# Attention head groups closed by VectorE straight out of PSUM, with the reciprocals and the last pass's preparing steps moved

## What is computed

```python
# layer 1, on x (8, 512, 512); 16 heads of 32
q, k, v = split(layernorm(x) @ w_qkv);  q, k = rotary(q), rotary(k)
attn = softmax(where(causal, q @ k.T / sqrt(32), -inf))
x = x + layernorm((attn @ v) @ w_o)
# layer 2, on z = layernorm(x)
h = z + attention(rmsnorm(z))        # latent keys and queries, again 16 heads of 32
out = h + moe(rmsnorm(h))            # 1 shared and 7 routed experts, top 2
x = x + layernorm(out)
```

## Time and profile before

| | |
|---|---|
| runs of the kernel before | 2252.98, 2257.77, 2262.41 us; median 2257.77 |
| the profiled execution | 2260.6 us, of which the span from first to last instruction is 2258.9 |
| PE busy | 2058.7 us (91%) |
| DVE, ACT, POOL busy | 1527.8 (68%), 1047.8 (46%), 1066.4 (47%) |
| attention stage | to about 1656 us of the span |
| mean granted clock of PE | 0.963 of full speed |

### The profile page before, as it was taken

How to read it: one execution, slowest core, us unless ns; L and a number is a source line. 1 busy time by engine, 2 the same in 40 slices (tenths; PEclk the granted TensorE clock), 3 DMA queues, 4 the chain that set the end, 5 groups by cost and what they waited for, 6 DMA issues and landing times. The chain is left out here.

```text
span 2258.9 us, 38261 instructions
## 1 busy us (share of the span) xinstructions
PE 2058.7 (91%) x12760; PEld 1471.1 (65%) x12760; DVE 1527.8 (68%) x4267; ACT 1047.8 (46%) x2154; POOL 1066.4 (47%) x1103
## 2 busy tenths in 40 slices
PE   5899989999998999999899999989689999999994
PEld 5676555767655576765557676555356778888883
DVE  5676777776666777666677776667646656565657
ACT  2345454443445444344543434454424355656554
POOL 1455654645555463555546455554525522323237
PEclk9999999999998999999899999989799999999997
DMA  5555556655545665555566555544446889999887
GB/s 174 172 138 150 151 150 178 188 135 139 160 140 150 177 189 133 140 158 143 150 168 197 149 143 153 147 113 117 136 164 243 282 233 241 214 225 234 218 238 258
DMA packets 227632, 394.74 MB, mean 175 GB/s; under 512 B 24942, under 2 KB 96238, under 8 KB 226158
## 3 DMA queue, kind: packets, MB, share of 16 engines
q1 hardware_dynamic: 164638, 294.69, 45.0%
q0 software_dynamic: 16064, 36.84, 8.8%
q10 hardware_dynamic: 46736, 60.77, 8.0%
HBM read 144.68 MB, written 146.35 MB: 129 GB/s over the span
## 5 line engine op out<-in xcount | busy, mean ns | idle before, releaser
L1044 DVE CUSTOM_DVE_ANT_0 unused<-score,mask 128x128 bf16<-128x128 f32 (+3 forms) x1024 | 468.3, 487 | 263.3 <-PE score L1280 245.6
L792 ACT ACTIVATE probs<-scoresT 128x512 f32<-128x512 f32 (+3 forms) x1024 | 426.5, 437 | 468.5 <-PE scoresT L1303 453.5
L1303 PE MATMUL scoresT<-stacks 97*128 97x256 f32 (+2 forms) x1024 | 399.0, 404 | 37.4 <-ACT probs L792 26.2
L697 POOL TENSOR_TENSOR probs<-probs 128x1536 f32<-128x1536 f32 (+1 forms) x128 | 375.1, 2931 | 34.1 <-PE out_ps L1317 24.8
L1280 PE MATMUL score<-stacks 96*128 96x256 f32 (+2 forms) x1024 | 347.9, 385 | 20.8 <-DVE rowmax L1044 17.8
L1162 PE MATMUL middle<-weights_by_part,xh 128*128 128x256 f32 x1792 | 343.9, 287 | 6.4 <-DVE weights_by_part L1013 4.6
L686 POOL TENSOR_SCALAR_AFFINE_SELECT probs<-probs 128x512 f32<-128x512 f32 x256 | 164.8, 644 | 345.1 <-ACT probs L792 345.1
L2510 PE MATMUL into<-xh,weights_by_part 128*128 128x512 f32 (+1 forms) x960 | 301.6, 382 | 4.5 <-PEq L468 2.4
L1162 PEld LDWEIGHTS middle<-weights_by_part,xh 128*128 128x128 f32 x1792 | 291.1, 192 | 17.6 <-DVE weights_by_part L1013 5.3
L1303 PEld LDWEIGHTS scoresT<-stacks 97*128 97x128 f32 x1024 | 195.5, 194 | 161.7 <-ACT probs L792 92.7
L1280 PEld LDWEIGHTS score<-stacks 96*128 96x128 f32 x1024 | 183.7, 195 | 152.8 <-issue 116.6
(11 more groups left out here) (233 smaller groups left out, 3242.5 us busy)
## 6 DMA issues: line engine op xcount, KB each, us to landing
stacks<-rows SPq DMA_DIRECT2D x768, 128.0 KB, 2.4
x_slots<-mask ACTq DMA_DIRECT2D x57, 1032.0 KB, 5.3
rows<-in_L_attn_x SPq DMA_DIRECT2D x16, 1024.0 KB, 5.8
weights_by_part<-parts_kept SPq DMA_DIRECT2D x7, 2048.0 KB, 8.8
raw<-in_gates SPq DMA_DIRECT2D x24, 512.0 KB, 6.7
raw<-in_ups SPq DMA_DIRECT2D x24, 512.0 KB, 5.9
raw<-in_downs SPq DMA_DIRECT2D x24, 512.0 KB, 6.8
rows<-x_slots SPq DMA_DIRECT2D x11, 1032.0 KB, 7.1
```

The costliest lines, as they stand in the source:

```text
L697: pool.tensor_tensor(probs[0][:, :, P * j:T], probs[0][:, :, P * j:T], probs[j][:, :, :], ALU.add)\
L792: act.activation(probs[j][:, h, 0:width], scoresT[:, u % ST_BANKS, first:first + width], ACT.Exp, scale=SCALE).then_inc(exp_done, 1)
L1044: ins = dve.tensor_tensor_reduce(unused[t][:, :], score.bank(name)[:, first:first + width], mask[:, T - width:T], 1.0, MASKED, ALU.add, AL ...
L1303: pe.matmul(scoresT[:, u % ST_BANKS, 0:T - first], heads[0:ROWMAX + 1, 1, h, j * P:(j + 1) * P], heads[0:ROWMAX + 1, 0, h, first:T], start ...
```

## The change

It does this:

- `O` and `CL` are gone, and with them `taken`, `whole`, `take_output` on ACT and `close` on POOL. `close` is now on DVE: one product of 128x512, `out_ps` by `total` into `outT`, right behind reciprocal 3. `close_last` takes `out_ps` for its four products too.
- The reciprocals are due at shares 0, 0.05, 0.10, 0.15 in every group. `PV` 0, 1, 2 move forward by 0.02.
- The next group's `PV` 0 and reciprocal 0 wait for DVE's product (`multiplied`) in place of `taken` and the old `out_done`.
- In pass 15: loading the first rows of h (`EF`) moves to the start of group 61; `EQ` 0 to the start of group 62, `EN` 0 after eight rooms, `EL` behind it; `EQ` 1 and `EN` 1 behind all of group 63's steps, ahead of its reciprocals.
- Just ahead of `PV` 2 of group 63, PE does the first three of four quarters of `Y` for row tiles 0 and 1.

```diff
@@ projections_between
+            if not starts:
+                steps = [("EF",)] + steps
@@
-            return [("EL",)] + [room] * AHEAD_AT[0] + [("EQ", 0)] + [room] * AHEAD_AT[1] + [("EN", 0)] + [room] * AHEAD_AT[2]
+            return [("EQ", 0)] + [room] * AHEAD_AT[0] + [("EN", 0), ("EL",)] + [room] * AHEAD_AT[1]
@@
-        steps += [room] * AHEAD_AT[3] + [*(("XT", p, k) for k in range(CT)), ("EQ", 1)] + [room] * AHEAD_AT[4]
+        steps += [room] * AHEAD_AT[3] + [("XT", p, k) for k in range(CT)] + [room] * AHEAD_AT[4]
         for k in range(CHUNKS):
             steps += [("EW", k), room]
-        steps += [("EN", 1)]
@@ head_group
-        steps += [(0.0, ("O", n - 1)), *((0.05 + (0.08 if n % NG else 0.04) * t, ("I", n - 1, t)) for t in range(TT))]
-    if n % NG > 0:
-        steps += [(0.45, ("CL", n - 1))]
+        steps += [(0.05 * t, ("I", n - 1, t)) for t in range(TT)]
@@
-    steps += [(share, ("PV", n, j)) for j, share in enumerate((0.37, 0.55, 0.74))]
+    steps += [(share, ("PV", n, j)) for j, share in enumerate((0.35, 0.53, 0.72))]
@@ attention_order
+            if step == ("PV", last, 2):
+                yield from quarters("Y", f, 0)[:3] + quarters("Y", f, 1)[:3]
+            yield step
+    yield from [("EQ", 1), ("EN", 1)]
     for t in range(TT):
-        yield "I", n, t
+        yield "I", last, t
     for t in range(TT):
-        yield from quarters("Y", f, t)
+        yield from quarters("Y", f, t)[3 if t < 2 else 0:]
@@ semaphores
+        def multiplied(n):
+            if n % NG == NG - 1:
+                return last_done, TT * (n // NG + 1)
+            return out_done, (NG - 1) * (n // NG) + n % NG + 1
@@ sync
+                def load_first():
+                    sp.wait_ge(h_stored, stores_of_h(max(opened(blocks)[:Ahead.OPENINGS]) + 1))
+                    sp.wait_ge(*middle.full(("XT", cores - 1, CT - 1)))
+                    sp.dma_start(normed[:, :, :], h_out[opened(blocks)[0]:opened(blocks)[0] + 1, :, :].rearrange(in_rows, p=P)).then_inc(qkv_in, 16)
@@ gpsimd: close and its call removed;  scalar: take_output and its call removed
@@ vector
-                        if n % NG > 0:
-                            dve.wait_ge(out_done, closed_by_pool(n))
-                        elif n > 0:
-                            dve.wait_ge(last_done, TT * (n // NG))
+                        if n > 0:
+                            dve.wait_ge(*multiplied(n - 1))
@@
+                def close(n):
+                    out_free(n)
+                    dve.wait_ge(inverted, TT * (n + 1))
+                    dve.tensor_tensor(outT[:, n % OUTS, :], out_ps[:, :], total[:, :], ALU.mult).then_inc(out_done, 1)
@@ close_last
-                    dve.tensor_tensor(outT[:, n % OUTS, mine], whole[:, mine], total[:, mine], ALU.mult)\
+                    dve.tensor_tensor(outT[:, n % OUTS, mine], out_ps[:, mine], total[:, mine], ALU.mult)\
@@
+                    if step == "I" and which[0] % NG < NG - 1 and which[1] == TT - 1:
+                        close(which[0])
@@ tensor, times_v
-                        pe.wait_ge(taken, n)
+                        pe.wait_ge(*multiplied(n - 1))
```

More of the change, by code:

```diff
@@ L271, in attention_order @@
     groups = NG * cores
+    f, last = cores - 1, groups - 1
     for n in range(groups):
-        yield from merged(head_group(n, groups), projections_between(n // NG, n % NG, cores))
-    f, n = cores - 1, groups - 1
-    yield "O", n
+        for step in merged(head_group(n, groups), projections_between(n // NG, n % NG, cores)):
+            if step == ("PV", last, 2):
+                yield from quarters("Y", f, 0)[:3] + quarters("Y", f, 1)[:3]
+            yield step
+    yield from [("EQ", 1), ("EN", 1)]
     for t in range(TT):
-        yield "I", n, t
+        yield "I", last, t
     for t in range(TT):
-        yield from quarters("Y", f, t)
+        yield from quarters("Y", f, t)[3 if t < 2 else 0:]
     yield "HS", f
@@ L374, in attention_layers @@
         total = sb("total", [P, T])
-        whole = sb("whole", [P, T])
         unused = [sb(f"unused{t}", [P, P * (t + 1)], BF16) for t in range(TT)]
@@ L443, in attention_layers @@
         sum_done = semaphore("sum_done")
-        taken = semaphore("taken")
         inverted = semaphore("inverted")
@@ L447, in attention_layers @@
         last_done = semaphore("last_done")
-        def closed_by_pool(n):
-            return (NG - 1) * (n // NG) + n % NG
+        def multiplied(n):
+            if n % NG == NG - 1:
+                return last_done, TT * (n // NG + 1)
+            return out_done, (NG - 1) * (n // NG) + n % NG + 1
         def half_turned(n, which):
@@ L588, in _ @@
                 for step, *which in order:
+                    if step == "EF":
+                        load_first()
                     if step == "EL":
@@ L698, in add @@
                         .then_inc(added, 1)
[L700 to L707, removed]
                 def scale_ahead(o):
@@ L735, in _ @@
                         x1_roots(*which)
-                    if step == "CL":
-                        close(*which)
             @block.scalar
@@ L793, in exps @@
                                    ACT.Exp, scale=SCALE).then_inc(exp_done, 1)
-                def take_output(n):
-                    if n % NG > 0:
-                        act.wait_ge(out_done, closed_by_pool(n))
-                    elif n > 0:
-                        act.wait_ge(last_done, TT * (n // NG))
-                    act.wait_ge(pv_done, TT * (n + 1))
-                    act.activation(whole[:, :], out_ps[:, :], ACT.Copy).then_inc(taken, 1)
                 def plain_keys(n):
@@ L862, in _ @@
                         take_high(*which)
-                    if step == "O":
-                        take_output(*which)
                     if step == "PV" and which[1] == 1 and which[0] <= NR * blocks:
@@ L1056, in invert, with out_free @@
                         dve.wait_ge(sum_done, n + 1)
-                        if n % NG > 0:
-                            dve.wait_ge(out_done, closed_by_pool(n))
-                        elif n > 0:
-                            dve.wait_ge(last_done, TT * (n // NG))
+                        if n > 0:
+                            dve.wait_ge(*multiplied(n - 1))
                     dve.reciprocal(total[:, mine], sum_ps[:, mine]).then_inc(inverted, 1)
+                def out_free(n):
+                    if n == 1:
+                        dve.wait_ge(parts_stored, 48)
+                    if n >= OUTS:
+                        dve.wait_ge(*middle.full(("Y", (n - OUTS) // NG, TT - 1)))
+                def close(n):
+                    out_free(n)
+                    dve.wait_ge(inverted, TT * (n + 1))
+                    dve.tensor_tensor(outT[:, n % OUTS, :], out_ps[:, :], total[:, :], ALU.mult).then_inc(out_done, 1)
                 def close_last(n, t):
                     mine = slice(t * P, (t + 1) * P)
[L1066 to L1069, removed]
                     if t == 0:
-                        dve.wait_ge(taken, n + 1)
+                        out_free(n)
                     dve.wait_ge(inverted, TT * n + t + 1)
-                    dve.tensor_tensor(outT[:, n % OUTS, mine], whole[:, mine], total[:, mine], ALU.mult)\
+                    dve.tensor_tensor(outT[:, n % OUTS, mine], out_ps[:, mine], total[:, mine], ALU.mult)\
                        .then_inc(last_done, 1)
```

2 lines of the change are left out of this document (removed).

## The result

The changed kernel took 2225.39 us (median of four runs, 2221.03 to 2232.09) against 2257.43 us for the kernel before in the same series (four runs, 2252.98 to 2262.41). The ratio is 0.9856, with a 95% interval of 0.9837 to 0.9875: 32 us faster, where 11 were forecast and 2229 us was the low end of the range. The profiled execution took 2225.16 us, 1.8 more than its span of 2223.4, against 2260.6 before. The expert stage is the same block as before (602.4 us against 602.3, from its first instruction on POOL to the end of the span), so the question is the attention stage alone. It ended 35.7 us earlier, at 1620.95 instead of 1656.61.

A forecast was written before the change was run, and what follows sets the result against it. The body was taken as bound by PE with small gaps, the stage's end by chains between engines. Body -3.1 and end -8.0 made -11.1 us, 2246.7 on the median, rounded to 2246; forecast 2238 to 2252, range 2229 to 2262.

The forecast's parts named there:

- ACT's copy: Body: removing 64 copies of 598 ns on ACT gains 1 us (bounds 0 and 5).
- POOL's product: Body: without 48 products on POOL the cut ends earlier and PV 2 waits less, 6.5 us gained (bounds 4 and 8).
- The clock behind it: Body: half clock behind three late PV 2, at most 3.4 us lost each; 3 us gained (bounds 0 and 10).
- Reciprocals: Body: earlier reciprocals gain 4 us at S (bounds 0 and 8); crowding DVE where projections are evacuated costs 2 (0 to 6).
- DVE's product: Body: 48 products on DVE cost 2.4 us at PV 0 in short groups and 1 us at first maxima.
- Where rows are renormalised: Second groups of passes 2, 6, 10, 14: reciprocals ahead of the last X1 lose 1.5 us each, 6 us (bounds 2 and 12).
- The end of group 62: Stage's end: EQ 0 at the group's start brings M and group 63's ST earlier; gain 4.2 us (2 to 6).
- Group 63: Stage's end: moving EQ 1 frees POOL and PV 2, 3, so reciprocal 0 starts earlier; gain 2.8 us (1 to 4).
- behind it: From reciprocal 0 to the last addition at the stage's end: 1 us gained (-6 to 1.3).
- The fear of half clock in the last quarters: Stage's end: PE idles 4 of 6 us, and at half clock eight quarters of Y take 7.2 us more.
- the full gain in the body: Rival: all three clock falls go, S gives 8, renormalising costs 2; body -20, end -8, 2230 us; chance 0.24.
- The slower rival: Second groups of passes 1, 5, 9, 13: last X1 over 2 us later, 10 us lost each; 2294 us; chance 0.06.

The follow-up runs named there:

- e11_after_copy: The changed kernel with 64 copies of 128x512, read by nobody, back on ACT under their old wait; ratio 0.9831 to the kernel before.
- e6_body_pool_work: The changed kernel with the old last pass and an unread 128x512 product on POOL at 0.45 of three groups in four; ratio 0.9951 to the kernel before.
- e1_tail: The kernel before with only the last pass's part of the change; ratio 0.9978, 5 us faster.
- e8_reciprocals_only: The kernel before with reciprocals due at 0, 0.05, 0.10, 0.15 and nothing else changed; ratio 0.9972, 6.3 us faster.
- e3_dve_product: The changed kernel with the old last pass, old reciprocal shares and old PV shares; ratio 1.0239 to the kernel before, 54 us slower.
- e9_pv0_only: The kernel before with only the first PV of each group due at 0.35 in place of 0.37; ratio 0.9946, 12 us faster.
- e4_product_late: The kernel before with POOL's product due at 0.57 of a group in place of 0.45; ratio 0.9954, 10.5 us faster.
- e10_pv12_only: The kernel before with PV 1 and 2 due at 0.53 and 0.72 in place of 0.55 and 0.74; ratio 0.9987.
- e5_body_old_pv: The changed kernel with the old last pass and PV back at 0.37, 0.55, 0.74; ratio 0.9921 to the kernel before, 17.8 us faster.
- e7_pv_only: The kernel before with only PV 0, 1, 2 moved to 0.35, 0.53, 0.72; ratio 0.9946, 12 us faster.
- e12_after_pv33: The changed kernel with PV due at 0.33, 0.51, 0.70; ratio 1.0022 to the kernel before.

## Why the prediction missed

By its own steps:

- **ACT's copy** (-1): right; `e11_after_copy` prices it at nothing that could be measured.
- **POOL's product** (-6.5 for the wait): right for what was counted. From group 2's to group 62's maxima, `PV`'s wait for POOL went from 7.8 to 1.2 us. But `e6_body_pool_work` puts POOL's time at about 16 us, since without the product's removal the earlier `PV`s wait 12.3 us rather than 7.8, and since 4 us of clock go with it. The terms of the sum were priced each against the kernel before, and not with the others made.
- **The clock behind it** (-3, bounds 0 and 10): this is the first term that was mis-sized. Busy time of PE fell by 16.3 us. The three falls like the one of the earlier trace rows's first row are gone, and each had a second one ahead of it that the prediction left out, 3.4 us of half clock besides the 6.8 (one that comes and goes: `e1_tail` has it at one place of the three). That seven places had the same wait and no fall was true, but it was no reason to take a third of the upper bound: these seven had no fall to lose, and all three others lost theirs. And the term looked only behind `PV`'s waits, while four falls, three of them of 13.7 us, stood where rows are renormalised. Of the 78 us at half clock, 31 went at the turns to passes 6, 10 and 14 and 20 at those four; 7 came up at two new places (361 and 890 us), which the prediction had named as a sign of being wrong.
- **Reciprocals** (-4 at `S`, +2 for crowding): right at `S`, which waited 7.6 us in place of 12.4. `e8_reciprocals_only` gave 6.3 us in all (2.5 to 10.4 by its interval), so the charge for crowding does not show.
- **DVE's product** (+3.4): right for the changed kernel. 48 products took 692 ns each, and `PV` 0 waited 1.0 us for them in all, 0.7 of it in group 62. But `e3_dve_product` shows the price that this term hid: 49.5 us of waits, had the reciprocals not moved. By the Trainium skill (SBUF — State Buffer, section Who interferes with whom) the product is free of POOL, as a VectorE instruction with at most one SBUF input does not contend with GpSimd. The trace agrees: all 48 took 690 to 694 ns, also the seven that had POOL busy beside them for over 640 of these, while the addition of `X1` (L1082), with both inputs in SBUF, took up to 1149.
- **Where rows are renormalised** (+6, bounds 2 and 12): this is the step that failed, in its sign. The stalls on ACT were to grow by 1.5 us at each place, as two more reciprocals would stand ahead of the last `X1`; they went from 1.62 and 1.35 us to 1.55 and 1.65, 0.2 more. The trace has one more ahead of it, not two (in pass 10 one at 1079.97 before, two at 1064.24 and 1066.58 after), and `XR` came 0.2 us later behind the maxima. And the prediction had moved `PV` 0 without asking which steps of PE it passes. It passes `XT`, whose wait for ACT went from 9.4 to 3.2 us, with half of the four long falls. `e9_pv0_only` gives 12 us for that one edit (8 to 16 by its interval; 10 in these four groups, 8 in the stretch from group 2 to 62), 14 to 18 away from the term as forecast. In the time line of the kernel after:

```profile
1068.44 0.49 PE L1297 MATMUL scoresT<-stacks 97*128 97x512 f32 x1 [1.55 <-ACT probs L790]
1070.58 1.88 PE L1297 MATMUL scoresT<-stacks 97*128 97x512 f32 x3 [1.65 <-ACT probs L790]
...
1073.77 1.94 PE L1311 MATMUL out_ps<-probs,V 128*32 128x512 f32 x8
1075.64 0.80 PE L1274 MATMUL score<-stacks 96*128 96x512 f32 x1
1076.23 1.06 PE L1149 MATMUL middle<-ident,rows 128*128 128x128 f32 x4
```

- **The end of group 62** (-4.2): measured -2.2, from group 62's maxima to the first `ST` of group 63. The chain went as described; the clock did not. The kernel after, then `e11_after_copy`, through group 62 and the start of 63:

```profile
1566.00:1594.00 28.00, 25.32 (x106) 13.12 (x107) 15.17 (x43) 12.49 (x28) 10.80 (x10) 0.51 0.54 168
```
```profile
1562.00:1590.00 28.00, 23.72 (x110) 12.60 (x111) 16.26 (x45) 14.51 (x31) 12.15 (x11) 0.70 0.58 176
```

  PE ran at half clock through nearly all of it (the sums took 2.36 us for 1.26). Where the clock was 0.70, group 63's maxima came 5.2 us closer to group 62's than before; in the changed kernel, 2.7. Why the clock fell there was not settled. It is not particular to the change: of the kernels with the old last pass, four with little else changed (`e4_product_late`, `e8_reciprocals_only`, `e9_pv0_only`, `e10_pv12_only`) had one fall of 31 us that began in group 62, where the kernel before had two of 6.8.
- **Group 63** (-2.8) and **behind it** (-1): measured -3.6 and -1.6. The lines that carry it, of the kernel after, against the earlier trace rows:

```profile
1598.37 5.21 DVE L1000 TENSOR_TENSOR weights_by_part<-raw,weights_by_part 128x512 fp32r<-128x512 f32 x5 [0.41 <-ACT weights_by_part L745]
...
1605.35 0.68 DVE L933 CUSTOM_DVE_ANT_0 turned<-rows 128x512 bf16<-128x512 f32 x1
...
1605.96 0.95 DVE L1046 RECIPROCAL total<-sum_ps 128x128 f32<-128x128 f32 x1
...
1611.51 7.13 PE L1336 MATMUL middle<-wo,outT 128*128 128x512 f32 x16 [1.85 <-DVE rows L1071]
```

  Reciprocal 0 starts straight behind `EQ` 1 and waits for nothing of PE's, as forecast. The fear of half clock in the last quarters was wrong: 7.13 us for 16 is full speed, in spite of 1.85 and 2.08 us of idle PE ahead of them.

The end gave 7.4 us for 8.0 forecast. That they lie so close is in part luck: group 62 gave 2.0 less than forecast, group 63 and what follows 1.4 more. The body gave 28.3 for 3.1. In the table of PE's waits from group 2's to group 62's maxima that is: `cut` -6.6, `XT` for ACT -6.2, `S` -4.1, DVE's queue ahead of `XT` -2.8, against +3.1 at ACT's exponentials and +3.6 at the maxima's DMA; with smaller ones the idle time fell by 12.2, and the clock gave the other 16.3. About half of the miss (12 us) is idle time, most of it the renormalising term; the other half (13 us) is the clock term.

Of the rivals, the full gain in the body (2230 us; its own terms add up to -18 in the body, not -20) was nearest, by the right reason for the falls, but with 2 us charged for the renormalising places where some were gained. The slower rival, 2 us more at passes 1, 5, 9, 13, did show a trace: these second groups each became 0.8 to 1.0 us longer, with no fall of the clock.

What stays open. Three kernels that share no edit (`e4_product_late`, `e5_body_old_pv`, `e7_pv_only`) each lose most of the falls at the turn to passes 6, 10 and 14, and `e1_tail` loses some of them with no edit there at all. Which gap decides is not shown, and how much of the 16.3 us of clock belongs to which edit is known only as far as the ratios tell. The half clock through group 62 has no cause shown.

## What to carry to other kernels

When a step's due time moves, write down which steps of the same engine it passes, and look in the time line whether one of them has a wait: ready work that moves ahead of a waiting instruction can be worth the wait and what the clock loses behind it, and the same work moved ahead of one that another engine stands for costs its own length there (1.94 us of PE, 2.13 us of idle ACT in `e12_after_pv33`). Such an edit is worth a run of its own: 0.02 of a group gave 12 us, and 0.02 more took 34 back. And before work goes to the engine that gates a buffer, look when it will be free there: with the same product on DVE the kernel was 18 us faster than before behind early reciprocals (`e5_body_old_pv`) and 54 us slower behind late ones (`e3_dve_product`).

## What the chip showed that was not expected

- The granted clock, not the waits, carried more than half of the body's gain. About 78 us of the body stood at half clock before, 34 after.
- Whether a wait costs the clock isn't told by its length. Behind 2.04 us of idle PE ahead of the transposes of `raw` at 1025.73 it fell in the kernel before; behind 2.03 at the same step it didn't in the kernel after (1016.80), nor in `e1_tail` (1028.27), whose steps there are those of the kernel before; nor did it behind 1.85 at 1611.51.
- Where PE stood for ACT twice (1.6 and 1.4 us) and a third time (1.37) a few us later, the half clock lasted 6.8 to 13.7 us, 37 to 48 us over four places; without the third wait 3.4 to 10.2 us, 24 to 27 over the four.
